# DLRM tower: the batch in quarters of 256 columns, and 56 of 120 pair groups turned so that VectorE sums them along rows

## What is computed

```python
e = jnp.stack([tbl_0[ids[:, 0]], ..., tbl_31[ids[:, 31]]], axis=1)   # 1024 x 32 x 64
left = jnp.einsum('bpd,pde->bpe', x[:, idx_i, :], W)                 # 496 pairs
z = jnp.sum(left * x[:, idx_j, :], axis=-1)                          # 1024 x 496
h = jnp.concatenate([z, dense_ctx], axis=1)
h = jnp.maximum(h @ W_top1 + b_top1, 0.0)
h = jnp.maximum(h @ W_top2 + b_top2, 0.0)
y = h @ W_top3
```

## Time and profile before

| | us |
|---|---|
| median of three runs | 507.48 |
| the profiled execution's own time | 505.64 |
| its span, first to last instruction | 503.7 |
| TensorE (PE) busy | 455.5 |
| VectorE (DVE) busy | 307.0 |
| GpSimd (POOL) busy | 246.3 |
| ScalarE (ACT) busy | 36.8 |

### The profile page before, as it was taken

One profiled execution on the slowest core, in us unless ns is written; L12 is line 12 of the kernel. 1 busy time (PEld: TensorE's weight loads), 2 busy tenths in 40 slices (PEclk: granted clock), 3 DMA queues, 4 the chain that ended last, 5 costly groups with the idle time before them and its releaser, 6 DMA issues.

```text
span 503.7 us, 5636 instructions
## 1 busy us (share of the span) xinstructions
PE 455.5 (90%) x2288; PEld 160.1 (32%) x2288; DVE 307.0 (61%) x295; ACT 36.8 (7%) x59; POOL 246.3 (49%) x266
## 2 busy tenths in 40 slices
PE   1025899999999999999999999999999999999998
PEld 0002233333333333233333333333333333233332
DVE  3002477767776777677712267767776777687700
ACT  2000000000000000000002100000000000000013
POOL 5777777777777760523377777755541000000000
PEclk9999799999999999999999999999999999999999
DMA  6999931111111310100011111111000000000000
GB/s 120 180 168 163 165 57 28 26 27 26 27 26 27 100 25 5 22 5 17 11 28 26 26 28 27 26 22 21 19 16 10 1 1 0 1 1 0 1 0 0
DMA packets 44605, 18.67 MB, mean 37 GB/s; under 512 B 39714, under 2 KB 40226, under 8 KB 44580
## 3 DMA queue, kind: packets, MB, share of 16 engines
q1 hardware_dynamic: 36068, 8.86, 13.8%
q0 software_dynamic: 8512, 9.45, 9.7%
HBM read 18.29 MB, written 0.00 MB: 36 GB/s over the span
## 4 chain that ended last, share of the span: by engine, by line
PE 85%; POOL 9%; issue 3%; DMA 1%; ACT 1%
PE left L419 48%; PE z_sum L435 25%; POOL gathered L270 9%; PE left L448 6%; PE xT L403 3%; PE left L460 3%; ACT z L352 1%; DMA gathered<-in_tbl_dram,ids_sb 1%; PE left L468 1%; DMA ids_sb<-in_ids_dram 1%; ACT h L380 0%
## 5 line engine op out<-in xcount | busy, mean ns | idle before, releaser
L322 DVE TENSOR_TENSOR products<-left,X 128x1024 f32<-128x1024 f32 x240 | 280.5, 1218 | 103.1 <-issue 76.6
L270 POOL DMA_INDIRECT gathered<-in_tbl_dram,ids_sb x256 | 241.8, 945 | 131.7 <-issue 75.7
L419 PE MATMUL left<-X,w_sb 64*128 64x512 f32 x1024 | 264.5, 620 | 0.0
L419 PEld LDWEIGHTS left<-X,w_sb 64*128 64x128 f32 x1024 | 98.3, 188 | 145.5 <-issue 77.2
L435 PE MATMUL z_sum<-products,ones_window 128*32 128x512 f32 x960 | 129.2, 599 | 3.3 <-ACT z L352 3.3
L316 DVE TENSOR_TENSOR diagonal<-left,X 64x512 f32<-64x512 f32 x32 | 22.2, 694 | 65.8 <-PE left L419 65.1
L435 PEld LDWEIGHTS z_sum<-products,ones_window 128*32 128x32 f32 x960 | 27.3, 109 | 93.7 <-issue 53.8
L403 PE MATMUL xT<-ident,gathered 128*128 128x128 f32 x128 | 22.8, 305 | 33.9 <-DMA gathered<-in_tbl_dram,ids_sb 33.9
L345 ACT ACTIVATE X<-xT 128x512 f32<-128x512 f32 x32 | 19.1, 598 | 331.8 <-PE xT L403 331.8
L435 PE MATMUL z_sum<-diagonal,diag_window 128*32 128x512 f32 x64 | 32.9, 601 | 2.4 <-ACT z L352 2.4
L403 PEld LDWEIGHTS xT<-ident,gathered 128*128 128x128 f32 x128 | 14.6, 150 | 58.6 <-DMA gathered<-in_tbl_dram,ids_sb 38.9
(11 more groups left out here) (18 smaller groups left out, 10.3 us busy)
## 6 DMA issues: line engine op xcount, KB each, us to landing
gathered<-in_tbl_dram,ids_sb POOLq DMA_INDIRECT x256, 2.5
w_sb<-in_W_top_dram SPq DMA_DIRECT2D x1, 512.0 KB, 7.3
w_sb<-in_L_rec_W_dram SPq DMA_DIRECT2D x1, 496.0 KB, 11.2
w_sb<-in_L_rec_W_dram SPq DMA_DIRECT2D x1, 480.0 KB, 11.5
w_sb<-in_L_rec_W_dram SPq DMA_DIRECT2D x1, 464.0 KB, 10.5
w_sb<-in_L_rec_W_dram SPq DMA_DIRECT2D x1, 448.0 KB, 10.7
w_sb<-in_L_rec_W_dram SPq DMA_DIRECT2D x1, 432.0 KB, 10.5
w_sb<-in_L_rec_W_dram SPq DMA_DIRECT2D x1, 416.0 KB, 10.7
```

The lines of the kernel that those rows point to most:

```text
L270: pool.indirect_dma_start(out=gathered[:, g % GATHERS, t, odd, :], out_offset=None, in_=tables[f], in_offset=bass.IndirectOffsetOnAxis(ap= ...
L322: nc.vector.tensor_tensor(products[:, G % PRODS, :, :], left[:, s, :, :], X[:, x_slot(h, k):x_slot(h, k) + 1, :].to_broadcast([P, 2, HB]), ...
L419: ins = nc.tensor.matmul(left[:, s, odd, :], w_sb[part, column:column + 2, :].rearrange("p a e -> p (a e)"), X[part, x_slot(h, m), :], sta ...
```

## The change

The batch is cut into four quarters of 256 samples. A group is done in one of two ways.

- Columns (64 groups of a quarter): as before, but with 256 samples two groups share one unit of work, so one slot holds four matmuls of 256 columns. VectorE multiplies the 1024 numbers of a slot in one instruction, and two window matmuls sum them. That is 32 units a quarter.
- Rows (56 groups of a quarter): X of m, 128 samples, is now the stationary operand, and eight matrices of W, 512 columns, the moving one. The result has the batch on the partitions. VectorE multiplies it with the gathered rows themselves and then sums it along the row with a `tensor_reduce` to 16 numbers in `z_nat`. A unit holds four groups for 128 samples; there are 28 a quarter.
- Own pairs: two units a quarter, each of 16 matmuls of 64 columns for eight values of m and 256 samples, multiplied and summed by VectorE like rows. The window sums of the own pairs and the zeros that padded them are gone.

A quarter thus has 62 units. At its end four transposes turn `z_nat` (with the context in its last 16 columns) into half of `z`; the other half comes from `z_sum`, now one chunk of 64 sums a quarter. The layers of a quarter run 10, 13 and 15 units into the next one, those of the last quarter at the end. All gathered rows of two quarters are kept (`rows`), so a quarter's gathers wait only for the multiplies of the quarter two before it. X for two field pairs is turned and copied together, six units ahead; in the first quarter the first four field pairs are turned before any work.

```diff
-    plan.append(("project", G))
-    ready = groups[max(G + 1 - REDUCE_LAG, 0)][2]
+        plan += [("x", n) for n in at.get(w, [])]
+        if w in stages:
+            plan.append(stages[w])
+        plan.append(("work", w))
+        if w and work[w - 1][0] != "columns":
+            plan.append(("rowsum", w - 1))
+        ready = 2 * sum(s <= w - LAG for s in slots)
+        if ready - sums >= TURN:
+            sum_up_to(sums + TURN)
...
+MLP_AFTER = {"zT": 6, "layer1": 10, "layer2": 13, "layer3": 15}
+    return [] if m > 11 else [12, 8] if m == 1 else [12, 7] if m == 0 else [12]
...
+            for q in range(QUARTERS):
+                if q >= 2:
+
+                    pool.wait_ge(multiplied, work_of_quarter[q - 2])
...
+                if x[0] == "rows":
+                    t, c = x[2] % (2 * QT), x[4]
+                    nc.vector.tensor_tensor(
+                        row_products[:, n % ROW_PRODS, :, :], left[:, s, :, :],
+                        rows[:, t:t + 1, 2 * D * c:2 * D * (c + 4)].to_broadcast([P, 2, BANK]),
+                        ALU.mult).then_inc(multiplied, 1)
...
+            def row_sum(w):
+                x, n = work[w], rows_before[w]
+                dve.wait_ge(multiplied, w + 1)
+                z_nat_free(dve, x[1])
+                if x[0] == "rows":
+                    column = 16 * ROW_UNITS.index(x[3:5])
+                    nc.vector.tensor_reduce(z_nat[:, x[2] % (2 * QT), column:column + 16],
+                                            row_products[:, n % ROW_PRODS, :, :].rearrange("p o (j d) -> p (o j) d", d=D),
+                                            AX.X, ALU.add).then_inc(row_summed, 1)
...
+                if x[0] == "columns":
+                    for g, (m, k) in enumerate(x[2]):
+                        for odd in (0, 1):
+                            ins = nc.tensor.matmul(left[:, s, odd, QB * g:QB * (g + 1)], weights(odd, m, k, 2),
+                                                   X[D * odd:D * odd + D, q % 2 * FP + m, :], start=True, stop=True)
+                elif x[0] == "rows":
+                    t, m, c = x[2] % QT, x[3], x[4]
+                    for odd in (0, 1):
+                        ins = nc.tensor.matmul(left[:, s, odd, :], X[D * odd:D * odd + D, q % 2 * FP + m, P * t:P * (t + 1)],
+                                               weights(odd, m, c, 8), start=True, stop=True)
                 else:
+                    for t in range(QT):
+                        for j in range(8):
+                            m = x[2] + j
+                            ins = nc.tensor.matmul(left[:, s, t, D * j:D * (j + 1)], X[0:D, q % 2 * FP + m, P * t:P * (t + 1)],
+                                                   w_sb[0:D, w_base(m) + 1, :], start=True, stop=True)
```

More of the change, by code:

```diff
@@ L56, with row_chunks @@
 W_COLUMNS = w_base(FP)
[L59 to L81, removed]
+def row_chunks(m):
+    return [] if m > 11 else [12, 8] if m == 1 else [12, 7] if m == 0 else [12]
@@ L90, in w1_rows @@
     return index
 def make_plan():
[L95 to L125, removed]
-        plan.append(("project", G))
-        ready = groups[max(G + 1 - REDUCE_LAG, 0)][2]
-        if ready - done >= TURN:
-            reduce_up_to(done + TURN)
@@ L130, in make_plan @@
[L130 to L133, removed]
+    work, begin = make_work()
+    batches, at = [], {}
+    for q in range(QUARTERS):
+        m = FP
+        for n in BATCHES.get(q, [2] * (FP // 2)):
+            fields = list(range(m - 1, m - 1 - n, -1))
+            m -= n
+            at.setdefault(max(begin[q, fields[0]] - X_AHEAD.get(q, 6), 0), []).append(len(batches))
+            batches.append((q, fields))
@@ new lines, in make_plan, with sum_up_to @@
+    slots = [w for w, x in enumerate(work) if x[0] == "columns"]
+    plan, sums = [], 0
+    stages = {begin[q, FP - 1] + n: (what, q - 1) for q in range(1, QUARTERS) for what, n in MLP_AFTER.items()}
+    def sum_up_to(n):
+        nonlocal sums
+        while sums < n:
+            plan.append(("sum", sums))
+            sums += 1
+    for w, x in enumerate(work):
+        plan += [("x", n) for n in at.get(w, [])]
[7 more added lines that the diff above has]
+            sum_up_to(sums + TURN)
@@ L136, in dlrm_tower @@
+    plan += [("zT", QUARTERS - 1), ("early", QUARTERS - 1)]
+    sum_up_to(2 * len(slots))
+    plan += [(f"layer{n}", QUARTERS - 1) for n in (1, 2, 3)]
+    return plan, work, batches
 def dlrm_tower(nc, dense_ctx, ids, tables, W, W1, b1, W2, b2, W3, w1_index, out):
-    plan, groups, units = make_plan()
+    plan, work, batches = make_plan()
     ctx = ExitStack()
@@ L198, in dlrm_tower @@
         slot, freed, use, mlp_banks = {}, [], 0, 0
+        begun = set()
+        turn = {}
         for what, n in plan:
-            if what == "project":
+            if what == "work":
                 slot[what, n] = use
@@ L326, in _ @@
             for what, n in plan:
[L327 removed]
+                if what == "work":
                     multiply(n)
+                elif what == "rowsum":
+                    row_sum(n)
         @block.scalar
         def _(act):
[L332 to L336 removed]
@@ new lines, in transpose_x @@
+            def transpose_x(n):
+                q, fields = batches[n]
+                if n == 0:
+                    pe.wait_ge(ident_ready, 1)
+                for m in fields:
+                    pe.wait_ge(rows_gathered[q % 2][m], 16 * 2 * QT * (q // 2 + 1))
+                turned_free(turn["x", n])
+                for m in fields:
+                    for t in range(QT):
+                        column = QB * (m - fields[-1]) + P * t
+                        ins = nc.tensor.transpose(turned[:, column:column + P],
+                                                  rows[:, q % 2 * QT + t, 2 * D * m:2 * D * (m + 1)], ident[:, :])
+                ins.then_inc(transposed, 1)
@@ new lines, in transpose_z @@
+            def transpose_z(q):
+                pe.wait_ge(context_loaded[q % 2], 16 * (q // 2 + 1))
+                wait_row_sums(pe, ROWS_IN_QUARTER * (q + 1))
+                turned_free(turn["zT", q])
+                for c in (0, 1):
+                    for t in range(QT):
+                        column = QB * c + P * t
+                        ins = nc.tensor.transpose(turned[:, column:column + P], z_nat[:, q % 2 * QT + t, P * c:P * c + P], ident[:, :])
+                ins.then_inc(transposed, 1)
```

460 lines of the change are left out of this document (255 added, 205 removed).

## The result

The changed kernel takes 528.78 us (median of 4, 523.9 to 529.64) against 506.47 us (median of 4, 504.24 to 507.76): a ratio of 1.0426, interval 1.0349 to 1.0502. It is 4.3% slower; 1.6% was forecast. The profiled execution took 528.31 us with a span of 526.5.

The account below looks back on a forecast made before the run. TensorE bounds the kernel before, VectorE the changed one: 53.3 start + 409.1 VectorE work + 27.6 layers + 6.2 own units + 15.6 end = 511.8 us span, 515.5 us forecast, 1.6% slower; range 488 to 542.

Parts of the forecast that it names:

- VectorE's price: Each multiply or row sum of 1024 numbers on VectorE costs 1.13 us; 368 instructions make 416 us.
- Rival B: Multiply and row sum on VectorE don't overlap, each instruction takes its whole 1.22 us: 33 us more, 548; chance 0.12.
- D's low row sum: Rival with both unknown prices low, row sum 1.08 us and own unit 2 us: 499 to 505 us; chance 0.10.
- The rule weighed there: On VectorE, the next instruction doesn't start until the pipe is empty; the prediction said the trace disagrees for multiplies.
- The layers: Inside a quarter, VectorE stands still 9.2 us (6.4, 0.7 and 2.1) while TensorE does the layers; three quarters, 27.6 us.
- Rival A: VectorE is fed without gaps as TensorE runs further ahead or its bursts are shorter: 482 us, up to 500; chance 0.20.
- The own unit's length: An own unit's 32 passes of 64 columns take TensorE 3.5 us, between 1.7 and 6.0.
- The start and the end: VectorE runs gapless from 53.3 us, behind the 32nd gather; 15.6 us remain behind the end of VectorE's work.
- The own unit at a quarter's end: TensorE needs 10.7 us against VectorE's 9.0: 1.7 us of wait in three quarters, 1.1 in the last, 6.2 in all.
- Rival C: TensorE's clock falls to 1.2 GHz at layer 1 and the own unit, about 9 us a quarter: 542 us; chance 0.08.
- TensorE's total: TensorE needs some 375 us over the kernel, against 455.5 busy before, with about 10 us for further tiling changes.

Follow-up runs that it names:

- layers_split: Changed kernel with layer 1 cut into its two ring slots and the layers spread over later units; 785.51 us beside 613.04 for the kernel before, on a disturbed chip.
- best1: Changed kernel with layer 1 and each own unit cut in two, layers later, no batch of X ahead in the first quarter; 503.3 us beside 506.06.
- filler: Changed kernel with the matmuls of the row units of m = 1 and 9 done twice, same result; 521.8 us beside 506.06 for the kernel before.
- own_wide3: Changed kernel with own-unit matmuls streaming 128 columns instead of 64, third run, on a sound chip; 524.08 us beside 506.04 for the kernel before.
- own_wide2: Changed kernel with own-unit matmuls streaming 128 columns instead of 64, second run, on a disturbed chip; 784.77 us beside 611.88 for the kernel before.
- best2b: best1 with the matmuls of the row units of m = 0, 1 and 9 done twice, on a sound chip; 504.02 us beside 506.04 for the kernel before.
- own_dense: Changed kernel with two matmuls of 512 columns instead of 16 of 64 per own unit, own pairs left out; 763.99 us beside 613.04, on a disturbed chip.
- own_wide: Changed kernel with own-unit matmuls streaming 128 columns instead of 64, first run, on a disturbed chip; 787.17 us beside 613.04 for the kernel before.
- act_sums2: best1 with 21 of the 112 row sums on ScalarE, 16 activations each; 505.91 us beside 506.04 for the kernel before, on a sound chip.

## Why the prediction was right or wrong

- **Direction.** Right, slower, and inside the range (488 to 542), if just above the 505 to 527 of the forecast itself. The size was not: 22.3 us of loss against 8 forecast (515.5 against 507.48).
- **VectorE's price.** Right. A row sum takes 1207 ns, and its successor starts 1.126 us after it; behind a multiply it is 1.13, whichever kind comes next. Rival B (each its whole 1.22) and D's low row sum are out, and so are the 0.065 us less that the prediction weighed for a row sum. The rule weighed there (the Trainium skill, "VectorE: DVE Perf Modes", "The DRAIN you can't avoid") was read too strictly: the section also says that a next instruction that isn't held starts earlier, and the trace agrees with that, 1.13 from start to start against a length of 1.21.
- **The layers.** Right: 6.61 + 0.66 + 2.18 = 9.45 a quarter against 9.2. Rival A (no gaps) is out. In layers_split and best1, with layer 1 cut in two, 6.4 and 7.0 of the 9.45 are left, so the length of the burst explains a part of the gap.
- **The own unit's length.** 3.7 us for 3.5. Right.
- **The start and the end.** 51.7 for 53.3, and 16.1 for 15.6. The terms named for the end add up to 17.7, not 17.9, which moves the forecast by 0.2.
- **The step that failed** is "The own unit at a quarter's end", and with it the first own unit, which stands in no term of the sum: TensorE's 10.7 us were added up at full clock. At full clock they do cost what was forecast (1.75 in filler, own_wide3; 0.57 + 0.65 at the last in own_wide2; none at the first in filler), 6.5 us in all. The changed kernel pays 21.3, so 14.8 us are the half clock's. That this is just the 14.7 missed is luck in part: the start came 1.6 us early, and the layers, the end and the full-clock price were 1.6 over together.
- **Rival C** had the mechanism (0.08) and the wrong place: it let layer 1 meet the slow clock, 9 us a quarter. In the changed kernel the clock stays up at the layers in all three quarters, and falls at own units outside them, for 5.0 us at first and 1.6 to 3.3 at each quarter's end. It should have been weighed at every burst that follows VectorE-bound work, and given more than 0.08. Its sign in the earlier trace rows was misread: the slice that shows 0.7 is the fifth, where TensorE is busy 80% or more; the half-idle one is the slice ahead of it, at 0.9. The clock fell behind the thin stretch, onto the work that followed, as it does at the own units.
- **TensorE's total** was put too low, 375 against 429.5 busy. A column or row unit takes 0.96 from start to start where the tiling alternates (182.54, 183.50, 184.46 in the changed kernel), not 0.86: 240 x 0.10 = 24 us, of which the forecast had 10 for all changes of tiling, and 17 more is half of the 34 us at half clock. The rest of the 54 us isn't worked out. It doesn't set the time, but TensorE had less slack than thought.

What stays open: why one quarter's end comes at half clock and the next doesn't in the same kernel (own_wide3, filler), and why a thinner stretch without an own unit (75.60:82.40) keeps its clock. The runs show that filling TensorE's half-idle stretches takes most of the slow clock away (best2b), that it also falls without narrow own passes (own_dense), and not whether those passes help it to fall.

## What to carry to other kernels

When the bound moves from TensorE to VectorE, price TensorE's bursts at either clock wherever its work ahead of them is thin: here eight sums took 1.86 us at full clock and 3.53 at half. At which of such places the clock falls couldn't be told beforehand from these runs. Make such bursts short and put them apart (own units cut in two, layer 1 in two parts): best1 did this and beat the kernel before, and doubled work that kept the clock up gave nothing on top (best2b). Before work goes to an idle engine, look at what is queued behind it there: ScalarE's 3.84 us held a copy that TensorE waited for.

## What was not expected of the hardware

- TensorE's granted clock falls to half for 3.4 to 10.2 us in a kernel that keeps TensorE busy 82% of the span, and with matmuls added for nothing its profiled span was 6.5 us shorter (one execution).
- On two chips the kernel before took 612 to 613 us and the changed one's variants 747 to 796. In the slow stretches of those variants TensorE's matmuls come 2.8 us apart, with the wait ahead of each put down to issue. Two rows of own_wide:

```profile
329.65 0.37 PE L526 MATMUL left<-w_sb,X 64*128 64x128 f32 x1 [2.43 <-issue]
332.45 0.37 PE L526 MATMUL left<-w_sb,X 64*128 64x128 f32 x1 [2.43 <-issue]
```

No run here shows the cause.
- A sum over 64 numbers on ScalarE, the ACTIVATE with its accumulator read, takes 0.24 us from one to the next (act_sums2), so a row sum there is 3.84 us against 1.13 on VectorE.
